# Graph attention in slots of two heads, shift on GpSimd, quotient before the back transposes

## The reference, cut to what matters

```python
def gat_layer(x, adj, W, a_self, a_neigh, b):
    feat = jnp.einsum('nf,hfo->hno', x, W)
    attn_self = jnp.einsum('hno,ho->hn', feat, a_self)
    attn_neigh = jnp.einsum('hno,ho->hn', feat, a_neigh)
    e = attn_self[:, :, None] + attn_neigh[:, None, :]
    e = jax.nn.leaky_relu(e, 0.2)
    e = e + MASK_VAL * (1.0 - adj)[None, :, :]
    alpha = jax.nn.softmax(e, axis=-1)
    out = jnp.einsum('hnm,hmo->hno', alpha, feat) + b[:, None, :]
    return jax.nn.elu(jnp.transpose(out, (1, 0, 2)).reshape(out.shape[1], -1))
# per graph: layer 0 on ctx (64 columns), layer 1 on its result (256); adj = layernorm(x)
shared = silu(x @ sw_gate) * (x @ sw_up) @ sw_down
```

## Time and profile before

| what | value |
|---|---|
| median of 3 runs | 578.97 us (572.78 to 579.12) |
| profiled execution | 580.78 us |
| its span, first to last instruction | 579.0 us |
| mean granted TensorE clock | 0.951 |
| busy: TensorE / VectorE / ScalarE / GpSimd | 499.9 / 354.3 / 277.9 / 214.2 us |

### The profile page before, as it was taken

How to read it: one execution, slowest core, us unless ns; L and a number is a source line. 1 busy time by engine, 2 the same in 40 slices (tenths; PEclk the granted TensorE clock), 3 DMA queues, 4 the chain that set the end, 5 groups by cost and what they waited for, 6 DMA issues and landing times.

```text
span 579.0 us, 10089 instructions
## 1 busy us (share of the span) xinstructions
PE 499.9 (86%) x3100; PEld 308.4 (53%) x3100; DVE 354.3 (61%) x1051; ACT 277.9 (48%) x700; POOL 214.2 (37%) x305
## 2 busy tenths in 40 slices
PE   3899999999729999778968799999989996988885
PEld 2545565555424426556746465666646643644553
DVE  5769977788743555655641645445464388388872
ACT  1447766766512334223564565256356355235651
POOL 1445656654322135545300533242243243213221
PEclk9999999999957999889987999999999999988995
DMA  9993000000000923987530000000000000000000
GB/s 221 345 235 123 3 1 2 2 2 19 20 36 1 225 93 83 238 196 169 119 104 0 2 1 1 1 0 0 0 0 0 0 0 1 0 2 19 10 18 29
DMA packets 34570, 33.59 MB, mean 58 GB/s; under 512 B 5888, under 2 KB 32864, under 8 KB 34272
## 3 DMA queue, kind: packets, MB, share of 16 engines
q1 hardware_dynamic: 30224, 28.14, 17.2%
q0 software_dynamic: 3072, 4.33, 4.1%
q10 hardware_dynamic: 1232, 0.60, 0.4%
HBM read 26.44 MB, written 6.62 MB: 57 GB/s over the span
## 4 chain that ended last, share of the span: by engine, by line
PE 66%; DVE 11%; issue 10%; ACT 8%; DMA 2%; POOL 2%; ACTq 0%; DVEq 0%; POOLq 0%
PE bank L944 6%; PE bank L919 6%; PE bank L956 5%; PE bank L618 5%; PE bank L724 4%; PE bank L934 4%; PE bank L966 3%; PE bank L603 3%; PE bank L1010 3%; PE bank L798 3%; PE bank L629 2%; PE bank L638 2%; PE bank L588 2%; PE bank L735 2%; PE bank L1030 2%
## 5 line engine op out<-in xcount | busy, mean ns | idle before, releaser
L2026 POOL TENSOR_SCALAR work<-work,R 128x256 f32<-128x256 f32 x128 | 59.0, 479 | 97.7 <-DVE R L1781 97.7
L1293 ACT ACTIVATE work<-bank,nmx 128x256 f32<-128x256 f32 x128 | 58.9, 472 | 50.7 <-DVE nmx L1769 50.7
L1963 POOL TENSOR_SCALAR work<-work,M 128x256 f32<-128x256 f32 x64 | 62.0, 971 | 38.9 <-DVE M L1500 38.6
L944 PE MATMUL bank<-work 128*128 (+1 forms) x128 | 60.3, 593 | 1.2 <-ACT work L1293 1.2
L1769 DVE TENSOR_REDUCE nmx<-bank 128x2 f32<-128x512 f32 x64 | 43.5, 689 | 26.9 <-PE bank L944 26.5
L1500 DVE CUSTOM_DVE_ANT_0 work<-bank,Nw 128x256 f32<-128x256 f32 x128 | 48.8, 418 | 9.2 <-PE bank L603 8.9
L1125 ACT ACTIVATE work<-bank 128x512 f32<-128x512 f32 x64 | 38.2, 596 | 26.8 <-PE bank L618 26.5
L618 PE MATMUL bank<-ident,work 128*128 128x128 f32 x256 | 43.5, 297 | 1.7 <-issue 1.6
L1118 ACT ACTIVATE bank<-bank 128x512 f32<-128x512 f32 x64 | 37.9, 592 | 8.0 <-PE bank L603 7.9
L956 PE MATMUL bank<-arena,kvb 128*64 128x256 f32 x256 | 34.9, 391 | 6.9 <-DVE arena L1760 6.8
L618 PEld LDWEIGHTS bank<-ident,work 128*128 128x128 f32 x256 | 30.6, 150 | 16.2 <-issue 15.4
(11 more groups left out here) (220 smaller groups left out, 974.1 us busy)
## 6 DMA issues: line engine op xcount, KB each, us to landing
work<-in_wg SPq DMA_DIRECT2D x16, 176.0 KB
work<-in_wu SPq DMA_DIRECT2D x16, 176.0 KB
work<-in_wd SPq DMA_DIRECT2D x16, 176.0 KB
ysum<-eoS SPq DMA_DIRECT2D x18, 128.0 KB, 9.5
arena<-in_wq SPq DMA_DIRECT2D x1, 2048.0 KB, 10.7
arena<-in_woT SPq DMA_DIRECT2D x1, 2048.0 KB, 17.1
arena<-in_kcqT SPq DMA_DIRECT2D x1, 1536.0 KB, 20.4
Pw<-in_w13T SPq DMA_DIRECT2D x4, 352.0 KB, 5.9
```

Of the source, the lines that this page charges most:

```text
L944: mm = pe.matmul(bank[t][:, :], qT[:, j, t * P:(t + 1) * P], kblk[:, bass.ds(b, 1), :, :].rearrange("p b h s -> p (b h s)"), start=True, s ...
L1293: act.activation(E2[:, j % 2, t, h, :], bank[t][:, h * S:(h + 1) * S], ACT.Exp, bias=nmx[:, j % 2, t, h:h + 1], accum_out=S2[:, j % 2, t, ...
L1963: pool.tensor_scalar(L[:, i % 4, 0, :], L[:, i % 4, 0, :], M[:, i % 4, 0:1], None, ALU.subtract).then_inc(d_ready, 1)
L2026: pool.tensor_scalar(E2[:, j % 2, t, h, :], E2[:, j % 2, t, h, :], R2[:, j % 2, t, h:h + 1], 1.0, ALU.mult, ALU.mult).then_inc(en2_ready, 1)
```

## The change

One slot `u` of the loop is now two heads (`PAIRS` = 32). Pair sums of a slot stand in one group: the second sums of the next slot's two heads and the first sums of the two heads after, over four PSUM banks (bank 7 is the fourth). Exp sums stand right behind the aggregation in the same slot. Both halves of the shift go to GpSimd, as a multiply by -1 and an add, and the exponential turns the sign back by its scale. VectorE takes the reciprocal of the sums (128 x 256) out of bank 4 and multiplies before the back transposes, which are then two instead of four, become a mix step in bank 5 and are copied by ScalarE. Mix steps come in two groups: `EARLY` ones at a slot's start, `LATE` ones ahead of the pair sums; VectorE and GpSimd take theirs in the same slot. Six shared products (`AHEAD`) move from behind the loop into its last slots, with their silu and product; `SHARED` begins with the ranks.

```diff
-TAIL = 24
+PAIRS = HEADS // 2
+TAIL = 13
-XB = (0, 1, 6)
+XB = (0, 1, 6, 7)
...
+    early, late = {}, {0: [("rows", 1)], 1: [("weights", 0)]}
+    for q in range(4 * B):
+        early.setdefault(2 * q + 6, []).append(("back", q))
     for k in range(1, 2 * B):
         if k > 1:
-            at.setdefault(GH * k - 10, []).append(("rows", k))
-        at.setdefault(GH * k - 4, []).append(("feat", k))
+            late.setdefault(4 * k - 5, []).append(("rows", k))
+        late.setdefault(4 * k - 2, []).append(("feat", k))
     for k in range(B):
-        at.setdefault(GH * k + 19, []).append(("hidden", k))
-        at.setdefault(GH * (k + B) + 22, []).append(("normed", k))
-        at.setdefault(GH * (k + B) + 23, []).append(("logits", k))
+        early.setdefault(4 * k + 11, []).append(("hidden", k))
+        late.setdefault(4 * (k + B) + 13, []).append(("normed", k))
+        late.setdefault(4 * (k + B) + 14, []).append(("logits", k))
...
+AHEAD = {PAIRS + 3 + i: w for i, w in enumerate([(what, n) for n in range(3) for what in ("gate", "up")])}
...
-    steps = [("gate", 0), ("up", 0), ("gate", 1), ("up", 1), ("rank", 0), ("gate", 2), ("cum", 0), ("up", 2)]
-    rest = [("down", 0), ("down", 1), ("gate", 3), ("down", 2), ("down", 3), ("up", 3)] + [("gate", 4), ("up", 4), ("gate", 5), ("up", 5)]
+    steps = [("rank", 0), ("gate", 3), ("cum", 0), ("down", 0)]
+    rest = [("down", 1), ("down", 2), ("down", 3), ("up", 3), ("gate", 4), ("up", 4), ("gate", 5), ("up", 5)]
+    rest += [("down", t) for t in range(4, 8)]
     for e, step in enumerate(rest):
         steps += [("count", e), step]
...
 # TensorE
+            def pair_sums(u):
+                if 0 <= u + 1 < PAIRS:
+                    pe.wait_ge(folded, 2 * (u + 1) + 2)
+                if u + 2 < PAIRS:
+                    pe.wait_ge(outer_ready, 3 * ((u + 2) // 4 + 1))
...
+                    if u >= 0:
+                        pe.wait_ge(masked, 4 * u + 4)
+                for t in range(TB):
+                    for i in (2 * u + 2, 2 * u + 3):
+                        if 0 <= i < HEADS:
+                            pair_sum(i, t, True)
+                    for i in (2 * u + 4, 2 * u + 5):
+                        if i < HEADS:
+                            pair_sum(i, t, False)
...
+            for u in range(-2, PAIRS + TAIL):
+                for what, k in EARLY.get(u, ()):
+                    mix_item(what, k)
+                if 1 <= u <= PAIRS:
+                    score_transposes(2 * u - 2)
+                    score_transposes(2 * u - 1)
+                if u % 2 == 1 and 3 <= u < PAIRS + 3:
+                    aggregate((u - 3) // 2)
+                if u % 2 == 1 and 3 <= u < PAIRS + 3:
+                    exp_sums((u - 3) // 2)
+                for what, k in LATE.get(u, ()):
+                    mix_item(what, k)
+                if u + 1 < PAIRS:
+                    pair_sums(u)
+                if u in AHEAD:
+                    what, n = AHEAD[u]
+                    shared_in(n, *((swg, 0) if what == "gate" else (swu, 2)))
...
 # ScalarE
-                act.activation(ET[:, q % 2, i % 4, :], bank[2 + i % 2][:, :], ACT.Exp).then_inc(e_done, 1)
+                act.activation(ET[:, q % 2, i % 4, :], bank[2 + i % 2][:, :], ACT.Exp, scale=-1.0).then_inc(e_done, 1)
...
+            for u in range(-2, PAIRS + TAIL):
+                for what, k in EARLY.get(u, ()):
+                    mix_item(what, k)
+                if u >= 10 and (u - 10) % 4 == 0 and (u - 10) // 4 < 2 * B:
+                    elu_below((u - 10) // 4)
+                if 1 <= u <= PAIRS:
+                    exponentials(2 * u - 2)
+                    exponentials(2 * u - 1)
+                for what, k in LATE.get(u, ()):
+                    mix_item(what, k)
+                if u + 2 < PAIRS:
+                    fold(2 * u + 4)
+                    fold(2 * u + 5)
+                if u >= 9 and (u - 9) % 4 == 0 and (u - 9) // 4 < 2 * B:
+                    elu_exp((u - 9) // 4)
+                if u - 2 in AHEAD and AHEAD[u - 2][0] == "up":
+                    shared_silu(AHEAD[u - 2][1])
...
 # VectorE
+            def aggregate_taken(q):
+                dve.wait_ge(agg_mm, q + 1)
+                if q >= 2:
+                    dve.wait_ge(mix_mm, MIX["back", q - 2])
+                link(dve.reciprocal(rinv[:, :], bank[4][:, S:2 * S]))
+                dve.tensor_tensor(aggS[:, q % 2, :], bank[4][:, 0:S], rinv[:, :], ALU.mult).then_inc(agg_evac, 1)
...
+            for u in range(PAIRS + TAIL):
+                if u < PAIRS:
+                    mask_and_max(2 * u)
+                    mask_and_max(2 * u + 1)
...
+                if u % 2 == 0 and 4 <= u < PAIRS + 4:
+                    aggregate_taken((u - 4) // 2)
+                for what, k in LATE.get(u, ()):
+                    if what == "rows":
+                        split_rows(k)
+                    elif what == "feat":
+                        feat_taken(k)
+                k, c = divmod(u - 10, 4)
+                if c == 0 and 0 <= k < 2 * B:
+                    elu(k)
...
 # GpSimd
-                pool.wait_ge(masked, 2 * i + 1)
-                pool.tensor_scalar(L[:, i % 4, 0, :], L[:, i % 4, 0, :], M[:, i % 4, 0:1], None,
-                                   ALU.subtract).then_inc(d_ready, 1)
+                for t in range(TB):
+                    pool.wait_ge(masked, 2 * i + t + 1)
+                    pool.tensor_scalar(L[:, i % 4, t, :], L[:, i % 4, t, :], -1.0, M[:, i % 4, t:t + 1],
+                                       ALU.mult, ALU.add).then_inc(d_ready, 1)
```

More of the change, by code:

```diff
@@ L314, in build @@
         d_ready = sem("d_ready")
-        d_second = sem("d_second")
         dT_done = sem("dT_done")
@@ L641, in exp_sums, with back_transposes @@
                 mm.then_inc(agg_mm, 1)
[L643 removed]
+            def back_transposes(q):
                 pe.wait_ge(agg_evac, q + 1)
[L646 removed]
+                mix_turn(("back", q))
                 for t in range(TB):
[L648 to L652 removed]
+                    mm = pe.transpose(bank[5][:, t * P:(t + 1) * P], aggS[:, q % 2, t * P:(t + 1) * P], ident[:, :])
+                mm.then_inc(mix_mm, 1)
             def hidden_transposes(k):
@@ L722, in shared_in @@
                     pe.wait_ge(shm_ready, n - 1)
+                else:
+                    pe.wait_ge(ld_sh, 16 * 2)
+                    pe.wait_ge(masked, 2 * HEADS)
+                    pe.wait_ge(e_done, HEADS)
+                pe.wait_ge(mix_evac, MIX["normed", 2 * c + 1])
                 for k in range(KT):
@@ L726, in shared_in, with mix_item @@
                 mm.then_inc(shg_mm, 1)
+            def mix_item(what, k):
+                if what == "back":
+                    back_transposes(k)
+                elif what == "rows":
+                    rows(k)
+                elif what == "weights":
+                    second_weights()
+                elif what == "feat":
+                    feat(k)
+                elif what == "hidden":
+                    hidden_transposes(k)
+                elif what == "normed":
+                    ln_transposes(k)
+                else:
+                    logits(k)
+            for u in range(-2, PAIRS + TAIL):
[15 more added lines that the diff above has]
+                    shared_in(n, *((swg, 0) if what == "gate" else (swu, 2)))
+            pe.wait_ge(mix_evac, len(MIX))
             def shared_down(t):
@@ L1181, in _, with mix_item @@
-            act.wait_ge(route_exp_in, B)
-            act.activation(prob[:, :, :], prob[:, :, :], ACT.Exp).then_inc(route_exp, 1)
+            def mix_item(what, k):
+                if what == "back":
+                    back_taken(k)
+                elif what == "rows":
+                    hi_part(k)
+                elif what == "weights":
+                    mix_taken((what, k), wrow[1][:, :, :].rearrange("p f c -> p (f c)"), bank[5][:, 0:KT * P])
+                elif what == "hidden":
+                    mix_taken((what, k), hT[:, k, :, :].rearrange("p f s -> p (f s)"), bank[5][:, :])
+                elif what == "normed":
+                    mix_taken((what, k), xlnT[:, :, k * S:(k + 1) * S],
+                              bank[5][:, :].rearrange("p (k s) -> p k s", k=KT))
+                elif what == "logits":
+                    mix_taken((what, k), Lp[:, k * TB:(k + 1) * TB, 0:E],
+                              bank[5][:, 0:TB * E].rearrange("p (t e) -> p t e", t=TB))
```

206 lines of the change are left out of this document (59 added, 147 removed).

## The result

The changed kernel took 589.93 us (median; 587.25 to 597.58), the kernel before 579.05 beside it: ratio 1.0187, 95% interval 1.0137 to 1.0236. That is slower: the interval lies above 1, though whether the loss is over two per cent is open. The forecast of "no change that could be measured" was 582.7, 7.2 us too low. The profiled run took 589.23 us (span 587.4), 8.4 more than the span of before.

A forecast was written before the change was run, and what follows sets the result against it. TensorE was taken as the loop's limit, with hand-overs setting the new period. Stretches -2.3 + 2.4 + 7.7 + 2.7 - 6.8 = +3.7 on 580.8 gave 584.5, by median level 582.7 us; range 573 to 592, overall 557 to 600.

The forecast's parts named there:

- (1): Second-layer period, ScalarE: two folds, elu exponential and back copy before bank 5 is free for the features; 2.1 us.
- (2): Second-layer period, TensorE: feature products and the first slot's pair sums behind them; 2.35 us.
- (3): Second-layer period, VectorE: feature evacuation and elu, partly beside the pair sums; 1.1 us.
- (4): Second-layer period, TensorE's second slot: hidden and score transposes, aggregation with exp sums, row products before pair sums; 4.35 us.
- (5) and (6): Second-layer period: hi copy 0.5 us, then VectorE's split until GpSimd starts 1.6 us.
- (7): Second-layer period, GpSimd: writing the outer rows; 1.75 us.
- (8): Second-layer period, GpSimd: the third slot's four shifts queue behind the outer rows; 2.2 us.
- Term (9): Second-layer period, TensorE's fourth slot: last score transposes, aggregation and exp sums, pair sums; 2.9 us.
- The clock falls within the loop: Rival: TensorE's clock falls once in each of four periods, +9 us, and +2 in the tail; 594 us, chance 0.18.
- TensorE stays the limit: Rival: hand-overs hide in the loop, a period takes about 14.0 us; 561 us in all, chance 0.28.
- GpSimd's shift costs as much as the old one: Rival: the loop's shift takes 0.97 us instead of 0.55, +12 us over seven periods; 595 us, chance 0.10.
- Shared products don't fill the tail: Rival: shared products stay behind the logits, +2.9 us; 586 us, its chance included in the forecast's 0.44.

The follow-up runs named there:

- rows_link: Changed kernel with the split's last two VectorE operations behind the next slot's masks and GpSimd's outer rows behind that slot's shifts; 575.53 us.
- loop_tail: rows_link with split's rest and outer rows another slot later, ScalarE's folds last, hidden transposes behind score transposes, third shared pair behind rank sums; 569.14 us, again 570.55.
- clock_fill: Changed kernel with eight more unused products in each period of eight heads, written where TensorE waits; 583.26 us.
- old_shared: Changed kernel with the shared network in its old place and order, no gate or up product ahead of the logits; 594.99 us.
- quotient_between: loop_tail with the small quotient back behind the back transposes, placed between the two heads' masks of its slot; 564.30 us, ratio 0.9758.
- shift_alone: Kernel before with only both shifts moved to GpSimd as multiply and add, exponential with scale -1; 584.7 us, ratio 1.0049.

## Why the prediction was right or wrong

**The number.** The time lies inside both ranges, 573 to 592 and 557 to 600, but "no change that could be measured" did not come out, and 582.7 came as near as it did partly by luck. Term by term the profile differs from the forecast by -2.6, +2.6, +3.8, +1.7, +2.3 and -3.0 us, which add up to 4.8; the rest of the 7.2 is that I counted a profiled run 1.8 above the median, and it was 0.7 below. By the prediction's own signs it was wrong in sizes and in one step: the period is 20.1 us and not 18 to 19, TensorE's work in it 15.13 and not under 14, the way from last logits to first count 9.8 and not under 8, and the clock of 0.50 ahead of the last aggregation, named there as a sign of being wrong, came.

**The chain of hand-overs: right.** For the period 98.65 to 118.62 the nine terms come out as follows, each from the end of the one before to its own. (1) folds, elu's exponential and back copy 2.1, predicted 2.1; (2) 2.33, predicted 2.35; (3) 1.05 and 1.1; (4) 4.39 and 4.35 (its parts as listed add up to 4.30); (5) and (6) 2.1 and 2.1; (7) outer rows 1.62 and 1.75; (8) shifts 1.86 and 2.2, since one takes 480 ns and not 550. That this chain, and not an engine's sum, set the period is shown by rows_link and loop_tail: at full clock and with 13.5 and 13.4 us of TensorE's work the period is 17.87 and 15.65, by program order alone.

**Term (9) failed, by a rival that was kept apart.** The last score transposes, aggregation, exp sums and pair sums took 4.5 us instead of 2.9, because the clock was at half rate for them. 19.97 - 18.85 = 1.1 is this 1.6 less 0.5 from (7) and (8). I had "The clock falls within the loop" as a case beside the forecast, at 0.18, with its own 594; it was the forecast's own consequence: where rows_link shortened the chain and where clock_fill filled it, the clock stayed at 1.00 in the loop. The prediction had even laid out the stretch, 2.7 us of work in 6.3, and then said that rows speak neither way. Adding the two gives 7.7 + 3 x 1.6 - 3 x 0.5, or 11.0 of the measured 11.5.

**Start and first two periods: right sum by luck, wrong terms.** -2.3 and +2.4 became -4.9 and +5.0. TensorE reached full rate earlier than in the kernel before, where exp sums at 37.48 still took 1.94. In the changed kernel those at 28.45 took 1.05, those at 38.48 again 1.94: it rose early and fell again in the first empty stretch. The first of the two periods took 15.6 us as predicted; the second took 20.6 and not 18.0, with two more falls of the clock in it (61.6 and 71.8 us).

**Tail: signs right, sizes off.** Ahead of the logits +4.4 instead of +2.7; behind them -4.5 instead of -6.8. The one gate product left there runs 3.54 us, not 1.98, again at half rate. I had the shared products gain 2.9 us on the way to the first count, 6.8 behind the logits less 3.9 for the third pair ahead of them; by old_shared they gain nothing there, 4.5 against 4.6. The -3.0 behind the first count, which I had put at nothing and -4 at best, went back in old_shared (391.0); but that stretch took from 382.6 to 386.1 in the seven kernels with the changed order there, and differs by 6 us between loop_tail and quotient_between, whose code there is the same. So its size and its cause stay open.

**Pair sums: right.** Eight products in four row groups take 0.40 us together, where four in two took 0.39; the assumption that they overlap held.

**The reciprocal: right.** 1.75 us predicted from the slope of the earlier trace rows, 1.753 measured. The Trainium skill (VectorE: DVE Perf Modes, "Walkthrough: the 8-slice pipeline in each mode") gives a repeat count of eight; read as eight cycles an element, as the prediction weighed it, that is an estimate of 2.1 us. The measurement, 6.8 ns an element, decides for less.

**Rivals.** "TensorE stays the limit" did not hold for this order, but a better one comes closer to it: 15.4 to 15.65 with 13.4 to 13.8 us of work. "GpSimd's shift costs as much as the old one" is refuted by 480 ns and by shift_alone. "Shared products don't fill the tail" is half right by old_shared: the products do run there, and behind the logits 4.5 us go, but the third pair costs as much ahead of them.

## What to carry to other kernels

Fewer, larger groups cut an engine's work, but they also put its partners' steps in series. Lay out the program order of every engine for one period, and add to its chain what the clock does in the stretch that the chain leaves empty: the two come together. When a step is off the time that its result is needed, put it behind the work that others wait for (split and outer rows: 12 us up to the first count for two moved loops), and ask of every operation put earlier what it waits for and who is queued behind it (the elu: nothing gained, 1.8 us of new wait). A saving on an engine that isn't the limit can show as nothing, as 2.4 us a period of VectorE did.

## What the runs showed of the hardware that was not expected

- The granted clock fell to 1.2 GHz in a period where no single wait of TensorE was over 1.1 us: ahead of the fall it had waited 0.81, 0.99, 0.91 and 0.29 us, with work between. With unused products in two of these waits (clock_fill) it stayed at 2.4 GHz.
- The same loop came out with a mean clock of 0.91 in one profile (the changed kernel, period 19.97) and 0.83 in another (old_shared, 20.50). What decides between them stays open.
- On GpSimd the shift as multiply and add takes 480 ns for 128x256 f32; the subtraction alone took 971. In the old order, in shift_alone, it takes 507. Two operations in one instruction took half the time of the single one.
